# Down-projections of chunk groups as seven-product blocks in the same pipeline, and sums of weights on GpSimd, in a one-core transformer layer

## The reference

```python
ffn_out = jax.nn.silu(hidden_states @ ffn_gate_w.T) * (hidden_states @ ffn_up_w.T) @ ffn_down_w.T
...
h1 = _lora_linear(x, w1, lora_A1, lora_B1)
h3 = _lora_linear(x, w3, lora_A3, lora_B3)
g = jax.nn.silu(h1) * h3
return _lora_linear(g, w2, lora_A2, lora_B2)
```

## Time and profile before

| | us |
|---|---|
| median of 3 runs | 455.64 |
| lowest and highest | 455.63, 456.31 |
| the profiled execution | 455.78 |
| its span | 454.1 |

### The profile page before, as it was taken

How to read it: one execution, slowest core, us unless ns; L and a number is a source line. 1 busy time by engine, 2 the same in 40 slices (tenths; PEclk the granted TensorE clock), 3 DMA queues, 4 the chain that set the end, 5 groups by cost and what they waited for, 6 DMA issues and landing times.

```text
span 454.1 us, 5522 instructions
## 1 busy us (share of the span) xinstructions
PE 448.8 (99%) x2033; PEld 368.5 (81%) x2033; DVE 301.3 (66%) x455; ACT 196.2 (43%) x302; POOL 17.2 (4%) x37
## 2 busy tenths in 40 slices
PE   9999999999999999999999999999999999999997
PEld 7788888888887878887888888878878778888786
DVE  5756799677865356776676238988862567887631
ACT  6364442355563124655444437365541124664300
POOL 1004000240000000000000000000000000000000
PEclk9999999999999999999999999999999999999999
DMA  8406100122101321122530010222201122111022
GB/s 294 132 0 189 62 1 0 37 80 66 51 1 46 94 69 46 48 69 67 148 101 35 17 48 16 70 66 52 79 4 41 54 92 65 46 56 62 1 94 91
DMA packets 16266, 29.42 MB, mean 65 GB/s; under 512 B 2224, under 2 KB 2496, under 8 KB 16240
## 3 DMA queue, kind: packets, MB, share of 16 engines
q1 hardware_dynamic: 14976, 27.01, 18.9%
q0 software_dynamic: 1264, 2.07, 1.7%
HBM read 26.97 MB, written 2.10 MB: 64 GB/s over the span
## 4 chain that ended last, share of the span: by engine, by line
PE 97%; DVE 2%; issue 1%; ACT 0%; DVEq 0%
PE PS L1281 18%; PE PS L1282 18%; PE PS L1283 18%; PE PS L1418 13%; PE PS L1419 13%; PE PS L1420 13%; PE PS L1510 1%; PE PS L1344 1%; PE PS L1295 0%; PE PS L1569 0%; PE PS L1579 0%; PE PS L1580 0%; PE PS L1523 0%; PE PS L1293 0%; PE PS L1567 0%
## 5 line engine op out<-in xcount | busy, mean ns | idle before, releaser
L1418 PE MATMUL PS<-HT,WU 128*128 128x512 f32 x266 | 104.4, 392 | 1.4 <-PE PS L1283 0.6
L1419 PE MATMUL PS<-HT,WU 128*128 128x512 f32 x266 | 103.7, 390 | 0.0
L1420 PE MATMUL PS<-HT,WU 128*128 128x512 f32 x266 | 103.5, 389 | 0.0
L1418 PEld LDWEIGHTS PS<-HT,WU 128*128 128x128 f32 x266 | 49.9, 188 | 14.2 <-issue 1.4
L1420 PEld LDWEIGHTS PS<-HT,WU 128*128 128x128 f32 x266 | 49.9, 188 | 10.6
L1419 PEld LDWEIGHTS PS<-HT,WU 128*128 128x128 f32 x266 | 50.0, 188 | 10.0
L400 ACT ACTIVATE WU<-raw 128x256 fp32r<-128x256 f32 (+2 forms) x48 | 42.1, 884 | 26.2 <-DVE raw L948 8.7
L773 DVE TENSOR_TENSOR WU<-raw,WU 128x256 fp32r<-128x256 f32 (+2 forms) x49 | 48.5, 995 | 5.4 <-ACT WU L400 5.2
L400 ACT ACTIVATE PS<-PS 128x512 f32<-128x512 f32 x38 | 22.1, 582 | 67.1 <-PE PS L1420 67.0
L1282 PE MATMUL PS<-G,DW 128*128 128x512 f32 (+1 forms) x122 | 47.1, 386 | 0.0
L1281 PE MATMUL PS<-G,DW 128*128 128x512 f32 (+1 forms) x122 | 47.1, 386 | 0.0
(11 more groups left out here) (171 smaller groups left out, 681.6 us busy)
## 6 DMA issues: line engine op xcount, KB each, us to landing
raw<-in_pieces SPq DMA_DIRECT2D x87, 256.0 KB, 2.7
X<-in_x SPq DMA_DIRECT2D x8, 256.0 KB, 5.2
out_x<-X SPq DMA_DIRECT2D x7, 256.0 KB, 2.0
su_raw<-in_stk_up POOLq DMA_DIRECT2D x6, 192.0 KB, 2.6
T<-in_lora_b POOLq DMA_DIRECT2D x16, 32.0 KB, 2.1
ga_raw<-in_lora_a POOLq DMA_DIRECT2D x8, 32.0 KB, 3.1
out_x<-X SPq DMA_DIRECT2D x2, 128.0 KB, 1.7
sm<-in_small POOLq DMA_DIRECT2D x1, 95.5 KB, 3.5
```

Source lines behind the costliest of these rows:

```text
L1418: pe.matmul(bank, w[:, 1, cols], xx[:, 0, :], start=start and kc == 0, stop=False, skip_group_check=not start)
L1419: pe.matmul(bank, w[:, 0, cols], xx[:, 1, :], start=False, stop=False, skip_group_check=not start)
L1420: mm = pe.matmul(bank, w[:, 0, cols], xx[:, 0, :], start=False, stop=kc == 1, skip_group_check=not start)
```

## The change

The first eight chunks' down-projections become block products too. Four chunks are a group: their G (512 units x 1024 tokens) is the moving operand, as a 2x2 block matrix, and 256 of the 512 outputs are one block's worth of weights, so a group is two blocks ("d", 42 matmuls each), and there are two groups per FFN. `BLOCKS` lists the order. Chunks from 8 on keep the ordinary way at the end (`down`), now 2 in FFN1 and 3 in FFN2. DW, `PHASES`, `half_step` and `pass_add` are gone; G grows by two slots.

The operands T1 to T4 of a group are sums of the G of its chunks. They are formed in three VectorE steps per pair of chunks (`g_sum` after an even and after an odd chunk, `g_sum4`), each with its own high and low parts: `g_hi` and `g_lo` have four events per pair instead of two. The outputs of a d block are added into X by `x_out` (four of 512 columns). The first d block of a pair begins with its own P1 (`enter_down`), since P1 is not done ahead in the block before. Corrections in FFN2 are made per block (`merge_block`) and for three full pieces.

The four sums of weights go from VectorE to GpSimd for all blocks, d blocks included (27 sets, 19 before). A set waits until low part 2 of the block before is written (and in FFN2 for the correction); the loads of a slot wait for the set too. The transfers of `lora_b`, issued by GpSimd, now come behind all sets of FFN1, and those of `stk_up` between the sets of FFN2.

```diff
-PHASES = (((0, 5), (5, 5)), ((0, 6), (6, 5)))
-CLASSIC = (0, 2)
...
+SU_AT = {6: 3, 8: 4, 12: 5}
...
+BLOCKS = ([("u", 0), ("u", 1), ("u", 2), ("u", 3), ("d", 0), ("d", 1), ("u", 4), ("u", 5), ("u", 6), ("u", 7),
+           ("d", 2), ("d", 3), ("u", 8), ("u", 9)],
+          [("c", 0), ("c", 1), ("u", 2), ("u", 3), ("d", 0), ("d", 1), ("u", 4), ("u", 5), ("u", 6), ("u", 7),
+           ("d", 2), ("d", 3), ("u", 8), ("u", 9), ("u", 10)])
+TAIL = (8, 8)
...
+        summed = {P_BLOCK[k][q]: fast(k, q) + 1 for k in range(2) for q in range(len(BLOCKS[k])) if kind(k, q) != "c"}
...
+                if before_in_slot(p) in summed:
+                    sp.wait_ge(sums_done, summed[before_in_slot(p)])
...
+            def sums(s, q):
+                p = P_BLOCK[s][q]
+                if s == 0:
+                    for k in range(2):
+                        pool.wait_ge(raw_in[SLOT[p + k]], raw_count(p + k))
+                else:
+                    pool.wait_ge(merged, q + 1)
+                if fast(s, q):
+                    prior = P_BLOCK[0][-1] if s and q == 2 else P_BLOCK[s][q - 1]
+                    pool.wait_ge(w_ready, prior + 2)
+                n = steps[0]
+                nc.gpsimd.tensor_tensor(sum_at("S1"), raws(q, "A21"), raws(q, "A22"), ALU.add).then_inc(sum_step, 1)
+                nc.gpsimd.tensor_tensor(sum_at("S3"), raws(q, "A11"), raws(q, "A21"), ALU.subtract).then_inc(sum_step, 1)
+                pool.wait_ge(sum_step, n + 1)
+                nc.gpsimd.tensor_tensor(sum_at("S2"), sum_at("S1"), raws(q, "A11"), ALU.subtract).then_inc(sum_step, 1)
+                pool.wait_ge(sum_step, n + 3)
+                nc.gpsimd.tensor_tensor(sum_at("S4"), raws(q, "A12"), sum_at("S2"), ALU.subtract).then_inc(sums_done, 1)
+                steps[0] = n + 3
...
+            for q in range(len(BLOCKS[0])):
+                sums(0, q)
+            pool.wait_ge(g_ready, event(0, 7, 3) + 1)
...
+            next_su(1)
+            next_su(2)
+            for q in range(2, len(BLOCKS[1])):
+                sums(1, q)
+                if q in (3, 7, 9):
+                    next_su({3: 3, 7: 4, 9: 5}[q])
...
-            def g_hi(s, c):
-                for h in range(HALVES):
-                    act.wait_ge(g_mul[h], unit(s, c) + 1)
-                copy(g_pair(s, c, 0), T[:, 2:4, :]).then_inc(hi_g, 1)
...
+            def g_hi(s, c, e=0):
+                if c >= TAIL[s]:
+                    for h in range(HALVES):
+                        act.wait_ge(g_mul[h], unit(s, c) + 1)
+                    hi = copy(G[:, 4 * (c - TAIL[s]) + 1:4 * (c - TAIL[s]) + 4:2, 0, :], T[:, 2:4, :])
+                elif e == 0:
+                    act.wait_ge(g_summed, 3 * (4 * s + c // 2) + 1)
+                    hi = copy(g_ops(c, B11, T1, 0), T[:, 2:7:4, :])
+                elif e == 1:
+                    act.wait_ge(g_summed, 3 * (4 * s + c // 2) + 2)
+                    hi = copy(g_ops(c, T2, 1, 0), T[:, 6:8, :])
+                elif e == 2:
+                    for h in range(HALVES):
+                        act.wait_ge(g_mul[h], unit(s, c) + 1)
+                    hi = copy(g_ops(c, B21, 1, 0), T[:, 2:4, :])
+                else:
+                    act.wait_ge(g_summed, 3 * (4 * s + c // 2) + 3)
+                    hi = copy(g_op(c, T4)[:, 0, :], T[:, 2, :])
+                hi.then_inc(hi_g, 1)
...
+            def steady(s, q):
+                part1_hi(s, q + 1, p4_done, fast(s, q - 1) + 1)
+                copy_bc(s, q, *c_free(s, q - 1))
+                g_first(s, q)
+                copy_e(s, q)
+                g_second(s, q)
+                part2_hi(s, q + 1)
+                fast_silu(s, q, 0)
+                g_third(s, q)
+                next_a(s, q)
+                fast_silu(s, q, 1)
+            def enter_down(s, q):
+                copy_ab(s, q, *b_free(s, q - 2))
+                part1_hi(s, q + 1, p4_done, fast(s, q - 1) + 1)
+                g_first(s, q)
+                copy_e(s, q)
+                g_second(s, q)
+                copy_ab(s, q + 1, *b_free(s, q - 1))
+                copy_bc(s, q, *c_free(s, q - 1))
+                part2_hi(s, q + 1)
+                g_third(s, q)
+            def blocks(s, q0, q1):
+                for q in range(q0, q1):
...
-                n = steps[0]
-                V.tensor_tensor(sum_at("S1"), raws(s, c, "A21"), raws(s, c, "A22"), ALU.add).then_inc(dve_step, 1)
-                V.tensor_tensor(sum_at("S3"), raws(s, c, "A11"), raws(s, c, "A21"), ALU.subtract).then_inc(dve_step, 1)
-                dve.wait_ge(dve_step, n + 1)
-                V.tensor_tensor(sum_at("S2"), sum_at("S1"), raws(s, c, "A11"), ALU.subtract).then_inc(dve_step, 1)
-                dve.wait_ge(dve_step, n + 3)
-                V.tensor_tensor(sum_at("S4"), raws(s, c, "A12"), sum_at("S2"), ALU.subtract).then_inc(sums_done, 1)
-                steps[0] = n + 3
-            def part1_lo(s, c):
...
+            def g_sum(s, c):
+                if c % 2 == 0:
+                    dve.wait_ge(g_mul[0], unit(s, c) + 1)
+                    dve.wait_ge(g_mul[1], unit(s, c) + 1)
+                    V.tensor_tensor(T[:, 6, :], T[:, 7, :], T[:, 2, :], ALU.subtract).then_inc(g_summed, 1)
                 else:
+                    dve.wait_ge(g_mul[1], unit(s, c) + 1)
+                    dve.wait_ge(g_ready, event(s, c, 0) + 1)
+                    V.tensor_tensor(T[:, 6:8, :], T[:, 3:4, :].to_broadcast([P, 2, N]), T[:, 6:8, :],
+                                    ALU.subtract).then_inc(g_summed, 1)
+            def g_sum4(s, c):
+                dve.wait_ge(g_ready, event(s, c, 2) + 1)
+                V.tensor_tensor(T[:, 2, :], T[:, 2, :], T[:, 6, :], ALU.subtract).then_inc(g_summed, 1)
...
+            def block_of(s, q):
+                up = is_up(s, q - 1)
+                c = chunk_at(s, q - 1) if up else None
+                if first_down(s, q):
+                    g_sum(s, c)
+                    mul0(s, c)
+                    part1_lo(s, q + 1)
+                    g_lo(s, c, 1)
+                    g_lo(s, c, 2)
+                    g_sum4(s, c)
+                    add_b(s, q)
+                    g_lo(s, c, 3)
+                else:
+                    if not up:
+                        x_out(s, q - 1, "c")
+                    else:
+                        mul0(s, c)
+                        if c < TAIL[s]:
+                            g_sum(s, c)
+                    part1_lo(s, q + 1)
+                    if up:
+                        g_lo(s, c, 0 if c >= TAIL[s] else c % 2)
+                        if c < TAIL[s] and c % 2:
+                            g_lo(s, c, 2)
+                            g_sum4(s, c)
+                    add_b(s, q)
+                    if up and c < TAIL[s] and c % 2:
+                        g_lo(s, c, 3)
+                if not is_up(s, q):
+                    x_out(s, q, "a")
+                add_d(s, q)
+                part2_lo(s, q + 1)
+                if s:
+                    merge_for(q + 2)
+                if is_up(s, q):
+                    mul1(s, chunk_at(s, q))
+                else:
+                    x_out(s, q, "d")
+                    x_out(s, q, "b")
...
+            def enter_down(s, q, after=nothing):
+                p1(s, q, *a_free(s, q - 2))
+                p5(s, q, copied_e, fast(s, q))
+                p1(s, q + 1, *a_free(s, q - 1))
+                p6(s, q)
+                p2(s, q)
+                p7(s, q)
+                after()
+                p3(s, q)
+                p4(s, q)
...
-            for c in range(1, 4):
-                fast_chunk(0, c, nothing, next_free=(silu[0], unit(0, c - 1) + 1))
-            fast_chunk(0, 4, nothing)
-            ready = [[(copied_e, 5), (silu[0], 5), (silu[1], 5), (g_mul[0], 5)],
-                     [(pass_added, 1), (silu[0], 4), (silu[1], 4), (pass_added, 4)]]
-            for n in range(9):
-                half_step(0, n, ready[n // 5])
-            p1(0, 5, pass_added, 2)
...
+            blocks(0, 1, 14)
             for h in range(HALVES):
-                for j in range(5):
+                for j in range(C1 - TAIL[0]):
                     down(0, h, j, down1_done)
```

More of the change, by code:

```diff
@@ L1008, in su_lo, with blocks @@
+            def blocks(s, q0, q1):
+                for q in range(q0, q1):
+                    if s and q in SU_AT:
+                        su_lo(SU_AT[q])
+                    block_of(s, q)
             def su_lo(q):
@@ L1423, in p1, with piece_ready, moving, fast_product @@
-            def p1(s, c, free, n):
-                piece_ready(s, c, 0)
+            def piece_ready(s, q, k):
+                pe.wait_ge(w_ready, P_BLOCK[s][q] + k + 1)
+            def moving(s, q, op, kc, part):
+                return HT[:, op, kc, part, :] if is_up(s, q) else G[:, 2 * op + kc, part, :]
+            def fast_product(s, q, weight, op, bank, start):
+                w, at = WU[:, wu_set(s, q)], OPERAND[weight][q % 2]
```

(43 more changed lines are left out.)

787 lines of the change are left out of this document (296 added, 491 removed).

## The result

The change makes the kernel slower: 463.34 us (median of 4 runs, 462.94 to 463.45) against 455.98 us for the kernel before, run beside it (4 runs, 455.63 to 456.50). The ratio is 1.0159, with an interval of 1.0141 to 1.0177. The prediction was 457.0 with a range of 449 to 463; the time lies 0.3 us above the range. The profiled execution took 463.45 us, its span is 461.7, so 7.6 more than before.

A forecast was written before the change was run, and what follows sets the result against it. The prediction took TensorE to bound the kernel, busy 448.8 of 454.1 us. Its sum was 455.8 - 10.9 (matmuls) - 2.7 (waits gone) + 11.4 (new waits) + 3.4 (GpSimd's sums) = 457.0 us, range 449 to 463.

The forecast's parts named there:

- TensorE's own work: Down-projections of both FFNs: 48 matmuls go at 0.227 us each, -10.9 us.
- Waits that go: TensorE waits at turns from blocks to half-passes and before the weights of FFN2's chunk 3 vanish, -2.7 us.
- Waits that come, without GpSimd: New TensorE waits from added VectorE and ScalarE work, taking GpSimd as harmless, +11.4 us in all.
- FFN1, two heavy blocks: Blocks after chunks 1 and 5, with extra VectorE sums of G: late bank B and next weights, 0.65 each, 1.3 us.
- FFN1, two entries: First d block of each down pair in FFN1: four waits, 1.45 us each, 2.9 together.
- turn to FFN2: From FFN1's last block to FFN2's opening low-rank product: late G and a long VectorE queue, 2.65 us.
- FFN2, first product block: VectorE still behind from the classic chunks: bank B 1.5 us late, next weights 0.4 late, 1.95 us.
- FFN2, two entries: First d block of each down pair in FFN2, with VectorE's correction on top: 1.1 us each, 2.2 together.
- rival 1: The handovers hold: 453.6 us if GpSimd disturbs nobody, 449.5 if the chains are also pessimistic; chance 0.35.
- GpSimd's sums: GpSimd's weight sums take turns with VectorE's two-SBUF-input operations: 0.55 us each, 4.4 at most, taken as +3.4 us.
- rival 2: GpSimd decides: its operations last 0.8 us or more and take turns with VectorE's, 461 to 466 us; chance 0.20.
- What would show it: Gaps of 0.3 us or more before P3 after chunks 1 and 5 and in entry blocks, 2 us opening FFN2.

The follow-up runs named there:

- e1: Changed kernel with each of GpSimd's four sums of weights handling 1 column instead of 256; 456.13 us, ratio 1.0007 to the kernel before.
- e12: Changed kernel with weights low part 1 first in pairs' first d blocks, G's later parts last after chunks 1 and 5, one-column GpSimd sums; 456.17 us, ratio 0.9998.
- e5: Changed kernel with the fourth S2 piece's high and low parts moved behind the other work of the turn to FFN2; 463.16 us, ratio 1.0159.
- e4: Kernel before with only its 19 sets of weight sums moved from VectorE to GpSimd; 455.72 us, ratio 0.9996.
- e7: Changed kernel with weights part 1 ahead of ScalarE's bank A copy and VectorE's first-half product in each pair's first d block; 462.15 us, ratio 1.0141.

## Why the prediction was wrong, point by point

**TensorE's own work: right.** The sum of its matmuls fell by 48, 10.9 us. **Waits that go: right**, none of the four in the earlier trace rows has a counterpart in the same place.

**Waits that come, without GpSimd: right in kind, 1.5 us short.** e1 is the measure. Its gaps beyond the pitch, with what the matmul behind each loses, and those of after, by place:

| place | sum | e1 | sum for the turns | after less e1 |
|---|---|---|---|---|
| FFN1, two heavy blocks | 1.3 | 1.65 | 1.0 | 0.85 |
| FFN1, two entries | 2.9 | 3.7 | 1.0 | 1.0 |
| turn to FFN2 | 2.65 | 2.5 | 0 | 0 |
| FFN2, first product block | 1.95 | 1.2 | 0.5 | 1.3 |
| FFN2, blocks ahead of an entry | 0.1 | 0.15 | 0 | 1.45 |
| FFN2, two entries | 2.2 | 2.5 | 1.4 | 1.45 |
| FFN2, heavy block | 0.3 | 1.0 | 0.5 | 0.7 |
| last block | 0 | 0.2 | 0 | 0 |
| together | 11.4 | 12.9 | 4.4, taken as 3.4 | 6.75 |

The chains that were played through in the prediction come out within 0.8 us at each place. Between the profiled executions of before and e1 another 1.1 us of gaps comes that the sum did not have; no single gap of it is over 0.2 us, and the gaps at FFN2's corrections are as large before (0.6 us together) as in e1 (0.5). So 453.6 became 456.1. Already this gives back the whole saving of 10.9 us: rival 1, the handovers hold, is refuted by e1, and e12 gives the same time in another order.

**GpSimd's sums: the step that failed.** The kind was right, turns at SBUF, and the size was wrong: the term was +3.4 and measured 7.2. First the length: 0.55 was taken, "near the lower end, since the nearest row is the same operation" on VectorE; it is 0.72 to 0.80 alone and about 1.0 in company. At the places where turns were counted, 5.3 us came instead of 3.4, about what the prediction's own scale gives for 0.7 (about 5), so the length can account for it; whether its deduction from 4.4 to 3.4, for waits of ScalarE, was right, the runs don't separate from that. The Trainium skill, GPSIMD Engine Reference, "Performance versus the Vector engine", leads to an estimate of 0.6 us for this operation; the trace says 0.72 to 0.80 without a collision, and the measurement decides. Second a place that was not seen, FFN2's two blocks ahead of an entry, 1.45. In FFN2 a set waits for the correction too, so it runs later in the block. VectorE, then GpSimd, of after:

```profile
382.31 1.21 DVE L1014 TENSOR_TENSOR T<-T 128x512 f32<-128x512 f32 x1
383.45 0.96 DVE L818 TENSOR_TENSOR WU<-raw,WU 128x256 fp32r<-128x256 f32 x1
384.65 1.43 DVE L818 TENSOR_TENSOR G<-T,G 128x1024 fp32r<-128x1024 f32 x1 [0.25 <-ACT G L465]
386.01 0.69 DVE L987 TENSOR_TENSOR PS<-PS,T 128x512 f32<-128x512 f32 x1
```

```profile
381.16 1.12 POOL L433 TENSOR_TENSOR raw<-raw 128x256 f32<-128x256 f32 x1 [8.32 <-DVE raw L1110]
382.24 0.73 POOL L434 TENSOR_TENSOR raw<-raw 128x256 f32<-128x256 f32 x1
382.94 1.19 POOL L436 TENSOR_TENSOR raw<-raw 128x256 f32<-128x256 f32 x1
```

The operations before `add_b` are 0.52, 0.54 and 0.20 us longer than alone, and this block, in which no P1 of the next stands ahead of P3, wants bank B six matmuls (1.4 us) earlier than others. That is the matmul at 386.75. FFN2's first product block has the same (1.3 instead of 0.5).

The last column leaves 0.5 of the 7.2 us. In the profiled execution of after the first four matmuls start 0.4 to 0.6 us apart, from 5.22 to 7.07, which costs 0.5 us against e1 and has nothing to do with GpSimd. Its three other executions show a mean granted clock of 0.996; e5 shows that this can leave 0.5 us of the same size, behind the wait that the turns have lengthened from 0.8 us (e1) to 2.1. So 6.75 us are the sums on GpSimd by place, and the rest is one or the other; where the clock fell in the three executions without a trace is not known.

**The rivals.** The time lies in the range of rival 2, GpSimd decides (461 to 466, chance 0.20), but that is in part luck. Its condition, operations of 0.8 us or more in turns, holds in company (about 1.0) and not alone (0.72 to 0.80). Its price was put as about 1 us more than the sum at each of eight places; the runs give it 7.2 - 3.4 = 3.8 in all, and the whole term is spread over ten places of 0.4 to 1.3 us each. The other 2.5 us above the forecast come without GpSimd. Its sign, gaps of over 2 us in every entry block, is missing: the largest gap of an entry is 1.0. Rival 1 is dealt with above. The sign had the largest chance (slower, 0.48), but 0.28 of that stood on losses of up to 460. The middle of rival 2's 461 to 466 is 463.5, not the 463 at which the range was closed; that moves the end of the range, not the cause.

**What would show it.** The gaps ahead of P3 after chunks 1 and 5 are there (0.73 and 1.3 beyond the pitch), and so is that at FFN2's opening (1.6 instead of 2). In the entry blocks of FFN1 the gaps of 0.3 or more stand ahead of the third (0.84), fourth (0.28, just under) and eighth product (0.63); the list named the second, though its working counts to the third (12 matmuls). The one in a light block, "a wait I have not seen", is there as well.

## What to carry to other kernels

Where a tuned pipeline hides VectorE and ScalarE behind TensorE with margins of tenths of a microsecond, a scheme that saves matmuls and pays with element work must be priced by the margin per block, not by the engines' mean load: here 10.9 us saved came back as waits (12.9 new, 2.7 old ones gone, 1.1 of small gaps) before GpSimd did anything. Work moved to GpSimd was not free for VectorE here, since it reads SBUF: where a block has no margin, count each of its operations, at its measured length, into VectorE's queue wherever two-input SBUF operations stand (7.2 us here); where it has 1.5 us of margin, as in the old blocks, the same sums cost nothing (e4). Of the reorderings tried only one gained, 1.2 us (e7); the others moved a wait without removing it, the sign of a full queue.
